# A graph layer with a routed feed-forward on one core: the first reads of x and of x transposed move from SP's queue to ACT's

## The reference, cut to what matters

```python
hn = layernorm(x)
A = adj - diag(adj);  d = diag(adj)
edge_output = gru(A @ hn, hn, edge weights)
for i in range(3):                              # heads
    hW = hn @ W[i]
    hp, hm = (A > 0) @ hW, (A < 0) @ hW
    e_plus, e_minus = leaky_relu([hp hm] @ a[i]), leaky_relu([hm hp] @ a[i])
    att = softmax over columns of (e_plus where A > 0, e_minus where A < 0, else -9e15)
    edge_support += att * A @ hW
node_output = gru(edge_support / 3, hn, node weights)
x = x + d * edge_output + d * node_output
x = x + ffn(layernorm(x))                       # 8 experts, the best 2 of each node
```

## Time and profile before

| | |
|---|---|
| median of 3 runs | 993.74 us (992.37 to 1000.39) |
| the profiled execution's own time | 991.16 us |
| its span, first to last instruction | 989.4 us |
| PE busy | 898.6 us, 91% of the span |
| DVE, ACT, POOL busy | 663.1, 650.0, 178.7 us |
| moved by DMA | 145.29 MB, mean 147 GB/s |

### The profile page before, as it was taken

One profiled execution on the slowest core, in us unless ns is written; L12 is line 12 of the kernel. 1 busy time (PEld: TensorE's weight loads), 2 busy tenths in 40 slices (PEclk: granted clock), 3 DMA queues, 4 the chain that ended last, 5 costly groups with the idle time before them and its releaser, 6 DMA issues.

```text
span 989.4 us, 9230 instructions
## 1 busy us (share of the span) xinstructions
PE 898.6 (91%) x2770; PEld 456.5 (46%) x2770; DVE 663.1 (67%) x1197; ACT 650.0 (66%) x855; POOL 178.7 (18%) x188
## 2 busy tenths in 40 slices
PE   5999999899798998999899899989989996588787
PEld 5634433356575443444344344434434442366642
DVE  6523332452688789779979977997998797242235
ACT  2345555611699879688887968888779773356532
POOL 0000000000002002000205400010570151256540
PEclk9999999999899999999999999999999998799999
DMA  9877766220279994996543232124212200665522
GB/s 287 308 252 276 243 245 242 98 88 17 50 225 209 197 221 113 191 182 109 133 170 107 95 111 100 56 95 171 104 47 103 81 30 0 172 202 170 153 101 119
DMA packets 105101, 145.29 MB, mean 147 GB/s; under 512 B 11708, under 2 KB 51446, under 8 KB 104918
## 3 DMA queue, kind: packets, MB, share of 16 engines
q1 hardware_dynamic: 101782, 137.90, 48.6%
q0 software_dynamic: 3264, 6.74, 1.9%
HBM read 122.02 MB, written 22.60 MB: 146 GB/s over the span
## 4 chain that ended last, share of the span: by engine, by line
PE 70%; DVE 18%; issue 5%; ACT 2%; another core or an unknown queue 2%; SPq 1%; DMA 1%; DVEq 0%; ACTq 0%
PE psum L2219 31%; PE psum L1965 15%; DVE big L1504 9%; PE psum L2049 4%; DVE work L1494 2%; PE psum L2316 2%; PE psum L2077 2%; PE psum L2304 2%; PE psum L2072 2%; PE psum L2073 2%; PE psum L2285 2%; PE psum L2113 1%; PE psum L1948 1%; PE psum L1904 1%
## 5 line engine op out<-in xcount | busy, mean ns | idle before, releaser
L2219 PE MATMUL psum<-big,h 128*128 128x512 f32 (+1 forms) x1092 | 463.9, 578 | 38.4 <-DVE big L1504 38.3
L1504 DVE TENSOR_TENSOR big<-work,big 128x1536 f32<-128x1536 f32 (+1 forms) x182 | 304.5, 1673 | 68.9 <-PE psum L2219 64.6
L2219 PEld LDWEIGHTS psum<-big,h 128*128 128x128 f32 x1092 | 208.3, 195 | 277.3 <-issue 201.7
L961 ACT ACTIVATE work<-work,shift 128x1536 f32<-128x1536 f32 (+1 forms) x182 | 268.4, 1475 | 27.4 <-DVE work L1494 24.9
L945 ACT ACTIVATE work<-rows,h 128x512 f32<-128x512 f32 x234 | 159.2, 712 | 16.2 <-DVE big L1504 14.7
L1965 PE MATMUL psum<-big,h 128*128 128x512 f32 x312 | 146.2, 611 | 0.0
L1494 DVE TENSOR_SCALAR work<-rows,h 128x512 f32<-128x512 f32 x234 | 111.1, 503 | 0.2
L1965 PEld LDWEIGHTS psum<-big,h 128*128 128x128 f32 x312 | 56.6, 192 | 68.6 <-issue 67.9
L755 POOL DMA_INDIRECT sorted_dram<-rows x44 | 68.7, 1562 | 98.4 <-DVE rows L1728 86.2
L719 POOL TENSOR_SCALAR_AFFINE_SELECT big<-big 128x128 f32<-128x128 f32 x50 | 17.2, 344 | 375.8 <-DMA big<-adj_cols_dram 373.5
L821 ACT ACTIVATE work<-big 128x2048 bf16<-128x2048 f32 (+1 forms) x42 | 75.0, 1785 | 12.1 <-POOLq L732 9.5
(11 more groups left out here) (293 smaller groups left out, 888.1 us busy)
## 6 DMA issues: line engine op xcount, KB each, us to landing
big<-adj_cols_dram SPq DMA_DIRECT2D x30, 2048.0 KB, 7.8
sorted_dram<-zeros SPq DMA_DIRECT2D x15, 910.0 KB, 19.2
big<-adj_cols_dram SPq DMA_DIRECT2D x9, 1024.0 KB, 7.4
big<-adj_cols_dram SPq DMA_DIRECT2D x6, 1536.0 KB, 6.7
rows<-stats_dram SPq DMA_DIRECT2D x12, 768.0 KB, 11.7
h_t<-experts_dram SPq DMA_DIRECT2D x17, 257.5 KB
rows<-sorted_dram SPq DMA_DIRECT2D x29, 130.0 KB
h<-experts_dram SPq DMA_DIRECT2D x12, 257.5 KB
```

The source lines that it names most:

```text
L961: nc.scalar.activation(place, place, ACT.Exp, bias=shift[:, 0:1], scale=-1.0).then_inc(g_e, 1)
L1504: nc.vector.tensor_tensor(wadj[:, n % 2, :, 0:w], wexp[:, n % SLOTS, :, 0:w], ring[:, place:place + 1, 0:w].broadcast_to([128, HEADS, w]), ...
L2219: done = nc.tensor.matmul(sums[i], h[:, t, 0:H], wadj[:, t % 2 if v == "plain" else 0, i, 0:w], start=t == 0, stop=t == TILES - 1)
```

## The change

The four issues of `x` and `x_t` leave SP's program and become ACT's first four instructions in the source, ahead of the square root. Their sizes, targets, semaphores and readers stay. On SP, `ident` now follows directly on the six small reads.

```diff
@@ sync engine
             for i in range(HEADS):
                 sp.dma_start(att_vec[:, i, :], gat_a[i].rearrange("(s p) o -> p (s o)", p=128),
                              allow_slow_non_contiguous=True).then_inc(gatw_in, 16)
-            for k, (t0, t1) in enumerate(((0, 8), (8, TILES))):
-                sp.dma_start(x_nodes[:, t0:t1, :], x[:, t0:t1, :])\
-                    .then_inc(x_in[k], 16)
-            for k, (t0, t1) in enumerate(((0, 12), (12, TILES))):
-                sp.dma_start(h_t[:, t0 * 128:t1 * 128], x_t[:, t0 * 128:t1 * 128]).then_inc(xt_in[k], 16)
             sp.dma_start(ident[:, :], ident_in).then_inc(ident_in_sem, 16)
@@ scalar engine
+            for k, (t0, t1) in enumerate(((0, 8), (8, TILES))):
+                act.dma_start(x_nodes[:, t0:t1, :], x[:, t0:t1, :]).then_inc(x_in[k], 16)
+            for k, (t0, t1) in enumerate(((0, 12), (12, TILES))):
+                act.dma_start(h_t[:, t0 * 128:t1 * 128], x_t[:, t0 * 128:t1 * 128]).then_inc(xt_in[k], 16)
             root(0)
```

## The result

The changed kernel's median is 999.57 us (22 runs, 996.61 to 1004.30). The kernel before, run beside it, now has a median of 995.33 us over 22 runs (989.88 to 1000.39), where the 3 runs known at the prediction had 993.74. The ratio is 1.0042, with a 95% interval of 1.0027 to 1.0057. In time that is 995.33 x 0.0042 = 4.2 us slower, 2.7 to 5.7. The forecast was +2.3 us and 996.0; so the direction is right and the size too small, and 999.57 lies just above the range's end at 999.0. Of that miss of 3.6 us, 995.33 - 993.74 = 1.6 is the base and 1.9 is the change itself.

The account below looks back on a forecast made before the run. PE's unbroken work from line 1904 was taken to bound the kernel. Late small reads would start it 2.3 us later, carried unchanged to the end: 996.0 us (+0.23%) on the base of 993.74, range 989.5 to 999.

Parts of the forecast that it names:

- What bounds the kernel: PE, busy without pause from line 1904 at 12.49 us; each microsecond earlier or later there is found again at the end.
- charge for a falling clock: PE idling 6.7 rather than 4.4 us before line 1904; if its clock drops for it, 1.9 us lost.
- Four issues on ACT: Start of ACT's program: four issues, 1.85 us, hidden in idle time; `x` and `x_t` issued 3.0 or 1.7 us earlier.
- What the data do: Opening reads: engines alternate queues by packet, so 88 short packets per engine outlast 32 long ones; `att_vec` lands near 11.9.
- `att_vec` lands near 11.9: Last small read: read when `x_t` is, about 11.1 + 0.1, landing some 0.7 us later, and not at 5.6.
- The sum: PE's start: line 1894 near 11.9, `w_att` ready at 14.6, line 1904 at 14.7 or 14.8, 2.3 us later than before.
- Is the rest still covered: DVE's features and chunk 0's masks keep 1.5 us or more of slack, chunk 1 doesn't bind; +2.3 us reaches the end.
- own range of +0.5 to +5: The main forecast's end time with table-load order, issue hindrance and clock drop as unknowns: 994.2 to 998.7 us.
- short packets slip through: Faster rival at the opening reads: small reads land near 5.6, line 1904 begins at 10.0, time 991.2 us; chance 0.3.
- the 9.8 that decides: Sign at the opening reads: `att_vec` landed before 12.49 - 2.7 = 9.8 us would mean the faster rival holds.
- chunk 0 takes the share of `x_t`: Slower rival at the opening reads: chunk 0 halves the rate of `x` and `x_t`, +1.5 to +2.5, 995.7 us; chance 0.08.
- it does nothing: Rival on the whole time: the shift at 12.5 is absorbed later or both effects cancel, 993.7 us; chance 0.12.

## Why the prediction was right and wrong

*What bounds the kernel* held: a shift of PE's line 1904 is found again, unshortened, as far as the start of the last stage. The charge for a falling clock was read from the wrong place: PE's idle time before line 1903 is 0.35 us and not 6.7, since nearly all of it now stands ahead of line 1893, and the granted clock stayed at 1.00 from 12.5 to 38 us.

*Four issues on ACT* held: they ran ahead of the table load, in 2.15 us rather than 1.85, hidden. SP's three `att_vec` issues took 2.03 rather than 1.47 while ACT issued too; this is small, and inside the sum below.

*What the data do* is the step that failed, in size. The mechanism was forecast, and from 5 to 12 us the counts show it (120 and 120, 110 and 110); the kernels with 8 and 16 small packets, the swapped queues and `x` in pieces exclude its rivals. The Trainium skill, in "DMA: Bandwidth & Descriptors", section "Queues, rings and completion order", has turns by packet, and the trace agrees from 5 to 12 us (385 and 394), though not from 4 to 6 (96 and 354). The same section has packets of about 9 to 17 descriptors as typical, where in that stretch each row of a read, from 4 to 9216 bytes, takes its own turn. The term "`att_vec` lands near 11.9" came out as 13.84, 1.9 us later, by two parts. First, the flow of `x` and `x_t` beside the small packets was put at 8.7 + 0.5 = 9.2 us, at the rate of a lone queue; it took from 1.9 to 12.5, 10.6 us, at 340 rather than 387 GB/s: +1.4. In part this is turns at a loss, as the 86% from 8 to 10 us show. Second, behind it 0.8 us were put for the rest and the landing, and it was 13.84 - 12.5 = 1.3: +0.5, since 284 short packets were left. The forecast had counted 88 packets against 32 as if the rest of the 88 cost nothing, though the earlier trace rows had their price: 771 of them took 1.8 us with no other queue beside them.

The rest of *The sum* held: 2.75 us from landing to line 1903 against 2.70. *Is the rest still covered* held too: DVE's features began at 24.51 and PE wanted them at 27.7; chunk 1 was with POOL at 32.88 and not 35.35, 2.5 us earlier as said, without deciding anything. To the 4.1 us at line 1903 come 0.3 in chunk 0's part, unexplained and not repeated in the second trace (4.3 and nothing more). So 4.1 + 0.3 = 4.4 and 4.5 at the landmark, beside the measured 4.2 (2.7 to 5.7). The own range of +0.5 to +5 held the shift; its end in time did not, because the base was a median of 3 runs.

*The rivals.* That short packets slip through is excluded: 13.84 against the 9.8 that decides. The Trainium skill, in "DMA: Bandwidth & Descriptors" under "Issuing engines are not separate DMA queues", has issuing from two engines save only issue time; here it moved the end by 4.2 us, the other way. That chunk 0 takes the share of `x_t` was not the cause here, since `x_t` landed before `w_att` was ready, but it is the likely reason in the kernel with the packed read, where `x_t` takes turns with 1 KB packets and its first half lands at 10.9 us, 0.7 later than in the changed kernel. That it does nothing is excluded by the interval.

## What to carry to other kernels

When transfers move to a second queue, count packets, not bytes. Beside long packets each DMA engine here gave both queues equal turns for most of the time, so a queue of many short packets lasted at least as long as the long packets beside it, and then the rest of the short ones took its own time; what waited on them was late by that. Before opening a second queue pack the small reads into few long rows. Here that was most of the gain: up to 176 us, at equal clock, 1.5 us for packing and 0.6 for the second queue after it, where without packing the second queue cost 4.2. The kernel with both has the lowest median of its chip (969.7 us beside 972.54 with packing alone and 973.2 before, ratio 0.9979), but a part of that is the clock's, see below. And look how far the next path is behind: PE could start 4 us earlier, and DVE took back most of it.

## What the hardware showed that was not expected

- Turns between two queues can cost rate: the engines were 86% busy from 8 to 10 us at 296 GB/s, where one queue gave 416, and 80% at 274 GB/s in the changed kernel's second trace. From 6 to 8 us, with the same one-for-one turns, they were full, at 407 GB/s; what makes the difference is open.
- A queue that begins behind 1 KB packets of another waited 4 us for its first packet, until a read of 1024 packets on the other queue was through, and within a microsecond had its equal turns.
- A read with tiles as the outer dimension came as 512-byte packets for 8 tiles and as 2048-byte packets for 18, unevenly done.
- PE's clock: over 296 to 336 us the kernel before and the changed one have a mean granted clock of 0.96, which is 2.4 GHz but for 40 x 0.04 x 2 = 3.2 us at the lower level, 1.2 GHz. Five of the eleven runs have 1.00 there: both packed kernels with the issues on ACT, the one on SP, the one in which ACT waits and the one with `x` in pieces. The packed kernel with `x` first, 2.0 us ahead at the landmark, is 3.8 ahead after this stretch and 5.4 at 836 us; from 470 to 500 us it has 1.00 too, where the kernel before has 0.94. The kernel with sixteen small packets is 2.2 ahead after this stretch and 2.3 at 836 us. The kernel with sixteen small packets stands at the same landmark (196.53 beside 196.57) and has 0.96, so the shift alone does not decide. The busy view (PE, PEld, DVE, ACT, POOL; clock, DMA share, GB/s) of the kernel before:

```profile
296.00:336.00 40.00, 36.55 (x110) 20.96 (x109) 33.44 (x43) 34.79 (x45) 5.25 (x7) 0.96 1.05 204
```

and of the packed kernel with `x` first:

```profile
296.00:336.00 40.00, 36.55 (x109) 20.13 (x108) 34.58 (x42) 36.90 (x47) 5.05 (x7) 1.00 1.10 214
```

PE is equally busy in both. No run here isolates what makes the clock fall. But two kernels that are level at the landmark are 3.1 us apart at 836, so part of the packed kernel's gain at the end goes with where the clock falls and not with its reads as such.
